# A decoder of two layers on one core: in the autocorrelation stage VectorE makes the remainder of the batch turned last at the head of its iteration, ahead of the sums

## The reference, cut to what matters

```python
x = _layernorm(x + _L0_attn_ref(...))            # masked dense
x = _layernorm(x + _L0_xattn_ref(x, ctx, ctx))   # autocorrelation: the stage of the change
x = _layernorm(x + _L0_ffn_ref(...))             # routed LoRA
...                                              # mixer, cross attention, LoRA

def _autocorrelation(Q, K, V):                   # per head, 64 features each, L = 128
    qf, kf = fft(q, axis=2), fft(k, axis=2)
    corr = ifft(qf * conj(kf), axis=2).real
    topk = int(2 * log(L))                       # 9
    w, idx = top_k(corr.transpose(0, 1, 3, 2), topk)
    w = softmax(w, axis=-1)
    for i in range(topk):
        g = minimum(idx[:, :, None, :, i] + pos, L - 1)
        out = out + w[:, :, None, :, i] * take_along_axis(v, g, axis=2)
```

## Time and profile before

| | |
|---|---|
| median of three executions | 2599.43 us |
| profiled execution, its time | 2601.73 us |
| profiled execution, its span | 2600.0 us |
| granted clock of PE, mean over the span | 0.98 |
| PE, DVE, ACT, POOL busy | 96%, 72%, 43%, 41% of the span |
| autocorrelation stage, first to last DVE instruction | 61.92 to 193.78 us |
| DVE iterations 3, 4, 5, 6 | 14.59, 14.59, 15.90, 14.97 us |

### The profile page before, as it was taken

How to read it: one execution, slowest core, us unless ns; L and a number is a source line. 1 busy time by engine, 2 the same in 40 slices (tenths; PEclk the granted TensorE clock), 3 DMA queues, 4 the chain that set the end, 5 groups by cost and what they waited for, 6 DMA issues and landing times. The chain is left out here.

```text
span 2600.0 us, 39171 instructions
## 1 busy us (share of the span) xinstructions
PE 2485.4 (96%) x14056; PEld 2038.8 (78%) x14056; DVE 1861.0 (72%) x2531; ACT 1125.2 (43%) x2660; POOL 1077.5 (41%) x889
## 2 busy tenths in 40 slices
PE   7878599999999999999999999989999999999999
PEld 4436488888888888888888888778888888888886
DVE  4865488697786986967859869656666666666675
ACT  2321334334343443343434433445556556565551
POOL 3011264555555546655555556633223223122223
PEclk9988799999999999999999999989999999999999
DMA  4000242131221321313213213111001001010100
GB/s 155 1 1 9 73 145 91 53 146 37 105 102 37 138 89 57 142 37 114 94 48 127 89 61 110 57 37 38 25 17 42 17 25 41 10 33 25 55 3 33
DMA packets 61555, 163.83 MB, mean 63 GB/s; under 512 B 8336, under 2 KB 8976, under 8 KB 52944
## 3 DMA queue, kind: packets, MB, share of 16 engines
q1 hardware_dynamic: 60144, 159.21, 17.8%
q10 hardware_dynamic: 1248, 2.36, 0.3%
HBM read 158.92 MB, written 2.62 MB: 62 GB/s over the span
## 5 line engine op out<-in xcount | busy, mean ns | idle before, releaser
L267 PE MATMUL pair<-XH,d_w_hi 128*128 128x512 f32 x1160 | 475.4, 410 | 29.1 <-POOL d_w_lo L1332 10.4
L268 PE MATMUL pair<-XL,d_w_hi 128*128 128x512 f32 x1160 | 463.0, 399 | 0.0
L269 PE MATMUL pair<-XH,d_w_lo 128*128 128x512 f32 x1160 | 462.4, 399 | 0.0
L1449 DVE TENSOR_TENSOR_SCAN d_decay<-d_decay,m_delta 128x1024 f32<-128x1024 f32 x128 | 359.9, 2813 | 13.7 <-DMA d_decay<-token_decays 12.3
L1351 POOL TENSOR_TENSOR d_decay<-d_decay,d_cb 128x1024 f32<-128x1024 f32 x128 | 309.6, 2419 | 136.4 <-DVE d_decay L1449 125.5
L1332 POOL TENSOR_TENSOR d_w_lo<-d_w,d_w_hi 128x512 fp32r<-128x512 f32 x144 | 187.9, 1308 | 284.2 <-ACT d_w_hi L1214 283.6
L267 PEld LDWEIGHTS pair<-XH,d_w_hi 128*128 128x128 f32 x1160 | 220.8, 190 | 87.9 <-issue 20.7
L1434 DVE SCALAR_TENSOR_TENSOR d_hs<-pair,d_conv,d_hs 128x1016 f32<-128x1016 f32 (+2 forms) x192 | 242.9, 1265 | 33.1 <-ACT d_hs L1239 28.6
L269 PEld LDWEIGHTS pair<-XH,d_w_lo 128*128 128x128 f32 x1160 | 220.4, 190 | 53.7
L268 PEld LDWEIGHTS pair<-XL,d_w_hi 128*128 128x128 f32 x1160 | 221.1, 191 | 47.6
L1356 POOL TENSOR_TENSOR d_gated_lo<-d_gated,d_gated_hi 128x512 fp32r<-128x512 f32 x128 | 173.6, 1359 | 157.4 <-ACT d_gated_hi L1258 157.4
(11 more groups left out here) (280 smaller groups left out, 6032.7 us busy)
## 6 DMA issues: line engine op xcount, KB each, us to landing
d_decay<-token_decays SPq DMA_DIRECT2D x64, 1024.0 KB, 4.9
d_w<-in_L_w_groups SPq DMA_DIRECT2D x144, 256.0 KB, 2.7
e_w<-in_L_w_heads SPq DMA_DIRECT2D x80, 256.0 KB, 2.7
d_wo<-in_L_wo_groups SPq DMA_DIRECT2D x64, 256.0 KB, 5.0
X<-in_x SPq DMA_DIRECT2D x8, 256.0 KB, 10.4
b_ctx<-in_ctx SPq DMA_DIRECT2D x8, 256.0 KB, 11.8
e_ctx<-in_ctx_t SPq DMA_DIRECT2D x4, 512.0 KB, 6.7
out<-X SPq DMA_DIRECT2D x8, 256.0 KB, 2.0
```

What stands on the lines that cost most here:

```text
L267: pe.matmul(out, wh, xh, start=first, stop=False)
L268: pe.matmul(out, wh, xl, start=False, stop=False)
L269: return pe.matmul(out, wl, xh, start=False, stop=last)
L1449: v.tensor_tensor_scan(r, r, m["DELTA"][:], 0.0, ALU.mult, ALU.add).then_inc(q["decay"], 1)
```

## The change

In DVE's loop the remainder of batch b-3 moves from behind `spectra(b+2)` to ahead of `sums(b-1)`. No instruction is added or removed; the other engines' code and every wait stay the same. It touches iterations 3 to 7.

```diff
                 for b in range(NB):
+                    if b >= 3:
+                        turned_lo(c, v, s, b - 3, c.bank[4])
                     if b:
                         sums(b - 1)
                     if b + 2 < NB:
                         spectra(b + 2)
-                    if b >= 3:
-                        turned_lo(c, v, s, b - 3, c.bank[4])
                     if b:
                         norm_apply(c, v, s, b - 1)
                     v.wait_ge(q["wf_ready"], b + 1)
```

## The result

The changed kernel took 2589.33 us, the median of five executions (2586.01 to 2592.16); the kernel before, in five executions, the three known before the prediction among them, 2601.17 (2597.91 to 2603.35). The ratio is 0.9952, 95% interval 0.9939 to 0.9966: 11.8 us faster by the medians, 8.8 to 15.9 by the interval. The forecast was 2591.3 us, a gain of 8.15 us, with a range of 2586.5 to 2596.5. The time lies within the range; the gain was put too low. The forecast took its 8.15 us off the median of three executions, 2599.43; taken off the median of five it gives 2593.0 us, so part of the closeness of the two times is luck. The profiled execution of the changed kernel is the one of 2589.33 us, with a span of 2587.6 us.

A forecast was written before the change was run, and what follows sets the result against it. The kernel was taken as 96% PE, this stage as a DVE and PE loop whose savings reach the end nearly unchanged. Gains in iterations 3 to 7 sum to 8.15 us, off the median 2599.43: 2591.3 us, range 2586.5 to 2596.5.

The forecast's parts named there:

- Where the wait was: Iterations 3 to 7: DVE's 12.8 us before its products and PE's 10.0 us for the remainder are one wait.
- What is late next: Iterations 3 to 5: DVE binds at 13.28 us, its norm ending with POOL's subtraction, 4.71 us behind the head.
- the other outcome: Iterations 3 to 5: with the norm at its free 0.54 us, each could gain some 0.6 us more.
- Terms: Gains by iteration: 1.31, 1.31 and 2.62 us in 3 to 5, 1.19 in 6, 1.72 in 7; sum 8.15.
- PE's lower clock was kept for iterations 6 and 7: Iterations 6 and 7: PE assumed at the lower clock, so products come 5.16 us behind the head.
- The last matmuls ... unchanged, 0: End of the stage: the last matmuls, the tail and all later stages were to gain 0.
- the favour: Rival: PE's clock at 1.00 throughout iterations 6 and 7 and the last matmuls; gain 12.8 us, time 2586.6; chance 0.13.
- No whole iteration ran at 1.2 GHz: Slower rival, iterations 3 to 7: a whole iteration at low clock costs up to 11.3 us; chance 0.04.
- no new wait for `exp` or `XH`: Signs of being wrong: `pick` beginning to wait for `exp`, or the head standing waiting for `XH`.
- The waits that I named as signs: Turn's waits for `XL` under 1.5 us; DVE's before products nil in iterations 3 to 5; 6 and 7 still await L542.
- One sign of being wrong: After this stage: any stage changing its length by more than 2 us would show the prediction wrong.

The follow-up runs named there:

- e1: Kernel before, with the remainder moved between the sums and the spectra instead of to the head; 2593.27 us, ratio 0.9970.
- e2: Kernel before, DVE's order kept, with PE's turn moved behind matmuls L541 and L542; 2588.73 us, ratio 0.9955.
- e3: Changed kernel, with POOL's subtraction of the next stage's weights moved ahead of the root; 2588.20 us, ratio 0.9949 to the kernel before.
- e7: Kernel before, unchanged, executed once more for a second profile; 2595.20 us in a single execution.
- e4: Kernel before, with the remainder moved to the head in iterations 6 and 7 alone; 2597.27 us, ratio 0.9986.
- e5: Changed kernel, with unread matmuls added on PE behind iterations 5 and 6; 2586.59 us, ratio 0.9942 to the kernel before.
- e6: Changed kernel, with both POOL's subtraction ahead of the root and unread matmuls behind iterations 5 and 6; 2585.96 us, ratio 0.9938 to the kernel before.
- e9: e6 with two more unread matmuls in each of three PE idle stretches at the stage's end; 2582.26 us, ratio 0.9929 to the kernel before.
- e10: e6 run again without edits, beside the changed kernel on the same chip; 2588.51 us, ratio 0.9951 to the kernel before.

## Why the prediction was right, and where its sum was short

- *Where the wait was.* Right: remainder, turn, L541, products are one wait. e1 shortens it as far as it brings the remainder forward (1.22 and 1.24 us), e2 removes it from the other end.
- *What is late next.* Right: in iterations 3 to 5 DVE binds, 13.24 us measured against 13.28, with the norm held by POOL until 4.71 us behind the head, to the hundredth. e3 shows that mechanism by itself, and that the 0.6 us an iteration, which I had named as the other outcome, was there to be had. One reading was off: in these iterations L541 starts 1.92 us behind the head, not about 1.5, as the weights it follows start 0.64 us behind it; 1.5 holds in iterations 6 and 7 (1.48 and 1.49). Its results were there ahead of the norm's end all the same.
- *Terms.* Iterations 3 to 5 gave 5.37 us (45.08 - 39.71) for 5.24, iteration 6 1.33 for 1.19, iteration 7 1.84 for 1.72: 8.54 for 8.15. Against this one profile of the kernel before they are right; against the other (e7) the same three are 7.1, 1.9 and 1.5, so that they fit so closely is in part luck. PE's lower clock was kept for iterations 6 and 7, rightly: 0.87 in iteration 6, and products 5.03 and 5.04 us behind the head for 5.16.
- *The term sized at nothing.* "The last matmuls ... unchanged, 0" is the step that was mis-sized, for the two profiles compared: 6.25 became 4.54 us, 1.71 us, as the clock was back at 1.00 for them. The third fall of the earlier trace rows, read there as 3.40 us, is part of one of some 10.3 us that reaches into the last matmuls; the changed kernel's, from 168.6 to 172.0, is over before them:

```profile
174.30:184.70 10.40, 8.16 (x13) 3.60 (x14) 4.21 (x8) 1.04 (x2) 0.79 (x2) 0.51 0.00 0
168.60:171.80 3.20, 3.20 (x7) 1.18 (x5) 1.49 (x4) 0.82 (x2) 0.79 (x2) 0.50 0.00 0
```

  The pieces behind gave 0.04 (59.95 to 59.91).
- *Why it is not a favour of one execution.* The error behind it: I took one profile's falls of clock for the kernel's. e7 has the last part at 4.54 us with the old code and pays 1.7 us more in iterations 3 to 5 instead; the sum is the same 133.1 and 133.3 us. The old order leaves PE idle 2.3 us five times and pays for some falls, now here, now there (three profiles of that code in iterations 3 to 5, with e4, all have one or two); the changed one has idle stretches only around iterations 6 and 7. So 10.4 us in the stage is the change's worth, 2.2 us over the forecast.
- *The rivals.* The median gain of 11.8 us lies nearer to the favour's 12.8 than to 8.15, but its condition did not come: the clock was not at 1.00 throughout iterations 6 and 7. Its 2.8 us for the last matmuls was too much besides: with the clock at 1.00 throughout (e5) they take 4.53 us from the products, 1.7 less than 6.25. No whole iteration ran at 1.2 GHz, none got slower, and no new wait for `exp` or `XH` came up. The waits that I named as signs behaved as said; DVE waits 0.33 and 1.27 us for L542 in iterations 6 and 7. One sign of being wrong, a later stage changed by more than 2 us, cannot be judged: "later" as a whole was 2.9 us shorter in the first pair, well within its scatter, so the sign was a poor one.
- *Open.* Whether the later stages add anything of their own. The first pair of medians gave 11.8 us, the last 10.4, the stage 10.4; with "later" scattering over 10.3 us and the interval of the first ratio 3.5 us to either side, differences of a few us cannot be told from such medians. Open too is what decides where a fall of the clock comes; that they come with PE's idle stretches is shown by what takes them away, the changed order in iterations 3 to 5 and the added matmuls in 6 and 7 (e5, e6, e9, e10).

## What to carry to other kernels

When an engine waits for an instruction that needs nothing late itself, look at what is queued ahead of it: here two matmuls stood behind a turn that waited for a leftover of an older batch, and one instruction moved by 2.8 us on another engine, or the turn moved behind them, freed both. Work out what binds next before moving on; it was an instruction that another engine's work held up. And take the places where PE's clock falls as a sample: profile the same kernel twice before crediting or charging a stretch with one.

## What the runs showed of the hardware that was not expected

Unread matmuls in PE's idle stretches paid: with those of e9 the clock was at 1.00 from iteration 6 through the start of the next stage, and the time from the last sum to the last remainder of that stage fell from 60.6 to 57.6 us. The same instructions in the same order met the lower clock in other iterations from one execution to the next (iteration 5 in one profile, 3 and 4 in two). The same code of the later stages took between 2342.6 and 2352.9 us in thirteen profiles.
